# Moving the next chunk's transposes between the key and the query product in the input stage of an adaLN attention and experts kernel

## What is computed

```python
h = _layernorm(x, axis=-1) * (1 + ca) + sa
x = x + ga * attention(h, Wq, bq, Wk, bk, Wv, bv, Wo, bo)
h = _layernorm(x, axis=-1) * (1 + cb) + sb
x = x + gb * experts(h, gate_w, gate_b, W1, b1, W2, b2)
```

## Time and profile before

| what | us |
|---|---|
| median of 3 runs | 2086.68 (2086.62 to 2087.52) |
| the profiled execution's own time | 2084.18 |
| its span, first to last instruction | 2082.4 |
| first key product of the stage starts at | 40.30 |
| eighth key product starts at | 134.34 |
| last query store of the stage is issued at | 147.18 |
| first load of the next stage is issued at | 151.33 |

### The profile page before, as it was taken

One profiled execution on the slowest core, in us unless ns is written; L12 is line 12 of the kernel. 1 busy time (PEld: TensorE's weight loads), 2 busy tenths in 40 slices (PEclk: granted clock), 3 DMA queues, 4 the chain that ended last, 5 costly groups with the idle time before them and its releaser, 6 DMA issues. The chain is left out here.

```text
span 2082.4 us, 47224 instructions
## 1 busy us (share of the span) xinstructions
PE 1842.0 (88%) x18361; PEld 937.0 (45%) x18362; DVE 456.9 (22%) x1360; ACT 1327.4 (64%) x1633; POOL 290.1 (14%) x329
## 2 busy tenths in 40 slices
PE   4863899999999999999999999665499999999995
PEld 3542333333333333333333333554266676767674
DVE  4655000000000000000000000345233333333331
ACT  2432789998999989999899999222133333333331
POOL 1000110001100011100010000365121212121211
PEclk9995899999999999999999999666699999999998
DMA  4336320000400004000000000863412121221223
GB/s 136 121 130 138 58 60 10 10 10 17 80 17 10 9 18 80 18 10 10 10 25 10 17 2 2 313 222 124 137 33 33 33 33 33 33 34 32 34 32 97
DMA packets 83823, 116.06 MB, mean 56 GB/s; under 512 B 9372, under 2 KB 75612, under 8 KB 83036
## 3 DMA queue, kind: packets, MB, share of 16 engines
q1 hardware_dynamic: 66616, 90.97, 15.4%
q0 software_dynamic: 13296, 17.80, 5.0%
q10 hardware_dynamic: 3760, 5.03, 0.9%
HBM read 73.03 MB, written 40.74 MB: 55 GB/s over the span
## 5 line engine op out<-in xcount | busy, mean ns | idle before, releaser
L1063 ACT ACTIVATE at_probs<-at_scores 128x1536 f32<-128x1536 f32 (+2 forms) x756 | 1023.0, 1436 | 57.9 <-PE at_scores L965 52.7
L965 PE MATMUL at_scores<-at_q_rows,kept_k_rows 99*32 99x512 bf16 (+3 forms) x9920 | 618.6, 363 | 34.6 <-ACT at_probs L1063 17.0
L982 PE MATMUL at_out<-at_probs,kept_v 128*17 128x512 f32 (+3 forms) x4832 | 587.6, 566 | 5.0 <-DVE at_out_T L1076 5.0
L965 PEld LDWEIGHTS at_scores<-at_q_rows,kept_k_rows 99*32 99x32 bf16 x9920 | 238.4, 96 | 560.7 <-ACT at_probs L1063 343.3
L1770 ACT ACTIVATE ex_hT<-ex_ps_hT,kept_b 128x128 f32<-128x128 f32 x568 | 154.2, 383 | 375.9 <-PE ex_ps_hT L1727 375.9
L1716 PE MATMUL ex_ps_h<-kept_w,ex_xT 128*128 x568 | 260.1, 601 | 0.9 <-DVE ex_xT L1785 0.9
L1735 PE MATMUL ex_ps_y<-kept_w,ex_hT 128*128 x1136 | 258.7, 381 | 2.5 <-ACT ex_hT L1770 2.5
L1076 DVE COPY at_out_T<-at_out 128x512 f32<-128x512 f32 x32 | 22.1, 691 | 972.0 <-PE at_out L982 972.0
L1735 PEld LDWEIGHTS ex_ps_y<-kept_w,ex_hT 128*128 128x128 f32 x1136 | 211.5, 191 | 28.9 <-issue 2.7
L1048 POOL TENSOR_SCALAR_AFFINE_SELECT at_probs<-at_probs 128x512 f32<-128x512 f32 (+2 forms) x156 | 83.1, 541 | 1010.0 <-ACT at_probs L1063 1008.4
L982 PEld LDWEIGHTS at_out<-at_probs,kept_v 128*17 128x17 f32 x4832 | 127.2, 98 | 131.1 <-DVE at_out_T L1076 20.3
(11 more groups left out here) (206 smaller groups left out, 928.2 us busy)
## 6 DMA issues: line engine op xcount, KB each, us to landing
kept_w<-in_W SPq DMA_DIRECT2D x16, 1024.0 KB, 9.8
ex_x_tile<-queue SPq DMA_DIRECT2D x72, 129.5 KB, 2.0
k_parts<-kparts SPq DMA_DIRECT2D x8, 768.0 KB, 3.7
q_parts<-qparts SPq DMA_DIRECT2D x8, 768.0 KB, 3.7
at_q_rows<-q_parts SPq DMA_DIRECT2D x32, 192.0 KB
kept_k_rows<-k_parts SPq DMA_DIRECT2D x4, 1120.0 KB
x_rows<-in_x SPq DMA_DIRECT2D x4, 1024.0 KB, 14.0
kept_k_rows<-k_parts SPq DMA_DIRECT2D x8, 512.0 KB
```

The lines of the kernel that those rows point to most:

```text
L965: ins = nc.tensor.matmul(ps_s[b:b + CT, c % 2, at:at + part], k_rows[:, k + b:k + b + CT], q_rows[:, q:q + part], start=True, stop=True)
L982: ins = nc.tensor.matmul(ps_o[h * CT:h * CT + HD + 1, first:C], v[:, kb, g * GH + h, :], probs[:, slot, column:column + width], start=i == ...
L1063: nc.scalar.activation(probs[:, c % RING, 0:width], ps_s[:, c % 2, 0:width], ACT.Exp).then_inc(exped, 1)
```

## The change

All loops over chunks are written out, 8 chunks each, with constant addresses and constant semaphore values, and the `sem_inc` calls ahead of them go (waits that they served are left out for the first chunks instead). On TensorE a chunk's turning moves one chunk ahead: chunk c + 1 is turned between the key and the query product of chunk c. On ScalarE the modulation of chunk c + 1 and then the normalising of chunk c + 2 come between keeping the key product and keeping the query product of chunk c; ahead of the chunks stand the normalising of chunks 0 and 1 and the modulation of chunk 0. VectorE's and SP's orders stay. No buffer is added, and every instruction that computes is issued as often as before. The new text, cut to its core (the removed lines are those of the four loops printed above):

```diff
+            for c in range(NC):
+                u = c % 2
+                for n, (parts, name, kept) in enumerate(
+                        ((kparts, "k_parts", k_stored), (qparts, "q_parts", q_stored))):
+                    sp.wait_ge(parts_ready, 2 * c + n + 1)
...
+            def normalise(c):
+                u = c % 2
+                if c >= 2:
+                    act.wait_ge(turned, c - 1)
...
+            def modulate(c):
+                u = c % 2
+                if c >= 2:
+                    act.wait_ge(v_ready, c - 1)
+                act.wait_ge(turned, c + 1)
...
+            def keep_one(c, n, full, ps, scale, bias):
+                act.wait_ge(k_ready, 2 * c + n + 1)
+                if c > 0:
+                    act.wait_ge(parts_ready, 2 * c - 1 + n)
...
+            normalise(0)
+            normalise(1)
+            modulate(0)
+            for c in range(NC):
+                keep_one(c, 0, kf, ps_k, 1.0, bk)
+                if c + 1 < NC:
+                    modulate(c + 1)
+                if c + 2 < NC:
+                    normalise(c + 2)
+                keep_one(c, 1, qf, ps_q, HD ** -0.5, bq_scaled)
...
+            def turn(c):
+                u = c % 2
+                pe.wait_ge(xn_ready, (c + 1) * CB)
+                if c > 0:
+                    pe.wait_ge(h_ready, c * KD)
...
+            def project(c, n_out, w, ps):
+                u = c % 2
+                pe.wait_ge(h_ready, (c + 1) * KD)
+                if c > 0:
+                    pe.wait_ge(kq_kept, (2 * (c - 1) + n_out + 1) * KD)
...
+            def values(c):
+                u = c % 2
+                pe.wait_ge(h_ready, (c + 1) * KD)
+                if c > 0:
+                    pe.wait_ge(v_kept, c)
...
+            turn(0)
+            for c in range(NC):
+                project(c, 0, wk_turned, ps_k)
+                if c + 1 < NC:
+                    turn(c + 1)
+                project(c, 1, wq_turned, ps_q)
+                values(c)
...
+            for c in range(NC):
+                split(c, 0, kf, kparts, k_stored)
+                split(c, 1, qf, qparts, q_stored)
+                dve.wait_ge(v_ready, c + 1)
```

More of the change, by code:

```diff
@@ L182, in _ @@
                          ones_rows[:]).then_inc(ones_stored, 16)
[L183 to L191, removed]
+            for c in range(NC):
[3 more added lines that the diff above has]
+                    sp.wait_ge(parts_ready, 2 * c + n + 1)
+                    to = dram[name][0:PARTS, :, c * C:(c + 1) * C]
+                    sp.dma_start(to.rearrange("(a d) h s -> (d h) a s", a=3 * KD),
+                                 parts[:, u].rearrange("p a m s -> p (a m) s")).then_inc(kept[u], 16)
             sp.wait_ge(ones_stored, 16)
             for u in range(2):
-                sp.wait_ge(k_stored[u], 16 * (NC // 2 + 1))
-                sp.wait_ge(q_stored[u], 16 * (NC // 2 + 1))
+                sp.wait_ge(k_stored[u], 16 * (NC // 2))
+                sp.wait_ge(q_stored[u], 16 * (NC // 2))
         @block.gpsimd
@@ L246, in _ @@
             act.wait_ge(act_step, 3)
[L248 to L277, removed]
@@ new lines, in normalise @@
+            def normalise(c):
+                u = c % 2
+                if c >= 2:
+                    act.wait_ge(turned, c - 1)
+                for j in range(CB):
+                    t = c * CB + j
+                    nc.scalar.activation(xn[:, u, j, :], x[:, t, :], ACT.Identity, scale=rstd[:, t:t + 1],
+                                         bias=shift[:, t:t + 1]).then_inc(xn_ready, 1)
+            def modulate(c):
[3 more added lines that the diff above has]
+                act.wait_ge(turned, c + 1)
+                for k in range(KD):
+                    nc.scalar.activation(hT[:, u, k, :], ps_turn[:, k, :], ACT.Identity,
+                                         scale=mod_cols[:, 2 + k:3 + k],
+                                         bias=mod_cols[:, k:k + 1]).then_inc(h_ready, 1)
@@ new lines, in keep_one @@
+            def keep_one(c, n, full, ps, scale, bias):
+                act.wait_ge(k_ready, 2 * c + n + 1)
+                if c > 0:
+                    act.wait_ge(parts_ready, 2 * c - 1 + n)
+                for m in range(KD):
+                    nc.scalar.activation(full[:, m, :], ps[:, m, :], ACT.Identity, scale=scale,
+                                         bias=bias[:, m:m + 1]).then_inc(kq_kept, 1)
+            normalise(0)
[8 more added lines that the diff above has]
+                keep_one(c, 1, qf, ps_q, HD ** -0.5, bq_scaled)
@@ L297, in _ @@
             pe.wait_ge(w_in, 16 * 6)
[L298 to L305, removed]
-                    for k in range(KD):
[L307 to L325, removed]
@@ new lines, in turn @@
+            def turn(c):
[3 more added lines that the diff above has]
+                    pe.wait_ge(h_ready, c * KD)
+                for k in range(KD):
+                    for j in range(CB):
+                        last = nc.tensor.transpose(ps_turn[:, k, j * P:(j + 1) * P],
+                                                   xn[:, u, j, k * P:(k + 1) * P], ident[:])
+                last.then_inc(turned, 1)
+            def project(c, n_out, w, ps):
[3 more added lines that the diff above has]
+                    pe.wait_ge(kq_kept, (2 * (c - 1) + n_out + 1) * KD)
+                for m in range(KD):
+                    for k in range(KD):
+                        last = nc.tensor.matmul(ps[:, m, :], w[:, k, m * P:(m + 1) * P], hT[:, u, k, :],
+                                                start=k == 0, stop=k == KD - 1)
+                last.then_inc(k_ready, 1)
@@ new lines, in values @@
+            def values(c):
[3 more added lines that the diff above has]
+                    pe.wait_ge(v_kept, c)
+                for j in range(CB):
+                    for k in range(KD):
+                        last = nc.tensor.matmul(ps_v[:, j, :], hT[:, u, k, j * P:(j + 1) * P], wv[:, k, :],
+                                                start=k == 0, stop=k == KD - 1)
+                last.then_inc(v_ready, 1)
+            turn(0)
@@ L381, in _ @@
             dve.wait_ge(w_in, 16 * 6)
[L382 to L412, removed]
@@ L413, in _, with split @@
-            dve.wait_ge(v_kept, NC + 1)
+            def split(c, n, full, parts, kept):
+                u = c % 2
+                dve.wait_ge(kq_kept, (2 * c + n + 1) * KD)
+                if c >= 2:
+                    dve.wait_ge(kept[u], 16 * (c // 2))
+                step.inc(nc.vector.tensor_copy(parts[:, u, 0], full[:]))
+                step.wait(dve)
+                step.inc(nc.vector.tensor_tensor(full[:], full[:], parts[:, u, 0], ALU.subtract))
+                step.wait(dve)
+                step.inc(nc.vector.tensor_copy(parts[:, u, 1], full[:]))
+                step.wait(dve)
+                nc.vector.tensor_tensor(parts[:, u, 2], full[:], parts[:, u, 1],
+                                        ALU.subtract).then_inc(parts_ready, 1)
@@ new lines, in _ @@
+            rows = bv_rows[:].rearrange("p (h d) -> p h d", h=H)
+            for c in range(NC):
+                split(c, 0, kf, kparts, k_stored)
+                split(c, 1, qf, qparts, q_stored)
+                dve.wait_ge(v_ready, c + 1)
+                nc.vector.tensor_tensor(v[:, c * CB:(c + 1) * CB, :, 0:HD],
+                                        ps_v[:].rearrange("p j (h d) -> p j h d", h=H),
+                                        rows.unsqueeze(1).to_broadcast([P, CB, H, HD]),
+                                        ALU.add).then_inc(v_kept, 1)
@@ L415, in over_tiles @@
+            dve.wait_ge(v_kept, NC)
 def over_tiles(eng, body):
```

## The result

The changed kernel takes 2075.49 us (median of 6 runs, 2070.80 to 2077.33), the kernel before, measured beside it, 2087.65 (6 runs, 2086.62 to 2089.61). The ratio is 0.9938, 95% interval 0.9925 to 0.9951: between 10.2 and 15.7 us faster, 12.2 by the medians. The forecast of 14.7 lies inside that interval: by the medians 2.5 us are missing, and the runs don't separate that from nothing. The profiled execution took 2075.32, 8.86 under the profiled one of before, so this pair lacks 5.8 of the forecast. In the pair the stages can be compared one by one, and the question is where these 5.8 us went.

What follows compares the result with a forecast made beforehand. The first stage was taken as bound by TensorE and ScalarE waiting for each other once per chunk. Saving 14.2 us over seven boundaries plus 0.46 at entry, 14.7, took 2086.68 to 2072.0; range 2070.5 to 2078.5.

Steps and rivals of the forecast that it cites:

- The bound and the cycle: First stage: TensorE and ScalarE in lockstep; turning between key and query product cuts the cycle from 13.22 to 11.19 us.
- What must hide: First stage: ScalarE's late keep of q costs nothing; TensorE's waits are met with 3.9 us to spare, VectorE's with 1.3.
- The entry: Before the first stage's chunk loop: without loop set-up ScalarE starts normalising earlier, 0.46 us saved; other bound 0.
- the clock of the first chunk: First key product: an earlier start may shorten or lengthen its slow spell, plus or minus 1.6 us at most.
- the first boundary: Between the first two chunks of the first stage: saves the same as the other boundaries, 2.03 us.
- The loops: First stage: removing three back edges gives nothing, as cycles with and without one are both 13.22 us.
- the 7.2 us of three fetches: First stage's back edges: three code fetches of 2.4 us would go if taken branches forced them; left out of the sum.
- The code grows instead ... I take 0: TensorE's written-out first stage: 480 more instructions, two code fetches, taken as 0 us; upper bound 4.8.
- The end simply moves: End of the first stage: the chunk does the same after the last key product, so the end only comes earlier.
- signs of being wrong: Key products over 12.5 us apart, TensorE waiting on "issue" in the first stage, or later stages with other lengths.
- The rival of the loop pushed out of place: Expert loop: longer code ahead makes each of 35 passes pay a 2.4 us fetch, 84 us, 2156; chance 0.05.
- Fetching eats a third: Rival, first stage: two extra code fetches each stall TensorE, 4.8 us in all, time 2076.8; chance 0.08.

Runs made afterwards that it cites:

- the second: The changed kernel measured and profiled once more, unedited: 2073.87 us, ratio 0.9935 against the kernel before.

## Why the prediction was right, and what it missed

**The bound and the cycle: right.** The stage was a lockstep of TensorE and ScalarE, and the new cycle is 11.20 against 11.19 forecast, turning 0.87 against 0.88. The dense stream of the expert stage was the right row to take it from; the bound of 1.13 was not needed.

**What must hide: right.** No new wait for TensorE; VectorE waits 0.5 for q where 0.8 was counted. Keeping q ahead of normalising changes nothing clear of the noise.

**The entry: right.** 0.49 saved (0.58 less 0.09) against 0.46. But the step "the clock of the first chunk", kept only in the range, cost 0.4 in the first profile (5.39 against 5.02) and 1.6 in the second (6.59). So the first boundary did not save "the same": 1.56 (14.71 to 13.15) instead of 2.03.

**The loops: right.** Equal cycles across and within back edges said that removing these would give nothing; written out in the old order the time is 1.0004 of before, and the 7.2 us of three fetches that the prediction weighed and left out were not there to be had.

**The sum: off by what stood outside the stage.** The step that failed is "The code grows instead ... I take 0". The mechanism was named and priced (two stalls of 2.4 us at most), but looked for in the wrong place. The prediction looked for the extra fetches where the code was added, at 7 instructions per us, and there TensorE never waits on issue. It took attention's good record (22 fetches in 200 us, one stop) as evidence that fetching is safe, and did not ask why that one stop stood where it did: 13 us behind the issue of a load of 3.1 MB. Longer code ahead moves the border of every later block. Counted against the kernel before with its loads spread, the kernel before loses 4.4 + 0.7 us at its one stop; the changed kernel's two cost 7.6, 8.1 and 7.6 in the three profiles of its TensorE code, net 2.5 to 3.0 us. That is the traces' figure; the times are too noisy to confirm it, since spreading the loads gained 4.1 us on the changed kernel (2073.87 to 2069.78) and 3.4 on the kernel before, each uncertain by about 3.

"The end simply moves" assumes that later stages keep their lengths. One of the prediction's own signs of being wrong therefore came true: attention is 3.6 us longer in the profiled pair, mainly 2.5 by the stops and 1.3 by the clock at tile 8, which is that one execution's. Without stops in either kernel its length agrees within 0.3.

The rival of the loop pushed out of place had the right idea, code moved by an earlier edit, but at the wrong stage: the expert loops take 568.2 us as against 567.8. The rival "Fetching eats a third" had the right mechanism, longer code that stalls TensorE, with two stalls in the stage where there is one stop more in attention: the gain of 12.2 lies as near to its 9.9 as to the 14.7 of the forecast.

**Luck.** That the time lies in the range is in part luck. The range's room above was counted for fetches in the stage that never came, and nobody chose where the borders fell: in one session the same order on TensorE measured 2073.87, with its code moved by a loop 2081.22, and with the loads spread 2069.78.

The rule of the Trainium skill, Runtime: NRT & Kernel Launch, section "Instruction fetch mechanics", that code is refilled in blocks of 256 instructions agrees with the runs: 64 and 80 instructions more moved the stop by 192 and 177 records. Its remark that the cost of crossing a border is mostly hidden agrees with the rest of attention, where no stop over 1 us stands; behind a key load these runs show stops of 1.9 to 3.9 us.

Open: score_shifts took 3.2 us less in the changed kernel's first profile, and attention started no earlier for it; nor were the 1.2 us behind attention looked into. What decides whether the clock falls behind a stop is not shown. What the single executions of one kernel differ by (2081 to 2093 for the kernel before in one session) was not traced.

## What to carry to other kernels

An engine that waits once per chunk for the one that it feeds is freed by putting the next chunk's preparation between two independent products of this one; price the moved work by the same instructions in a dense stream, not by how long they take beside a gap. Code written out is moved code: everything behind it meets its block borders elsewhere, and a border that is reached 13 to 16 us behind the issue of a load of 3 MB stopped the engine here, so spread large loads that nobody needs yet. When a stage gains what it should and the total doesn't, align the two traces by an event that recurs to the end, and look for the one step in the differences.

## What the runs showed of the hardware

The profile counts TensorE's code among the packets of the same 16 DMA engines as data. With 3.1 MB issued ahead of it, a fetch that otherwise comes some 9 us behind the last came 17 to 20 us behind it, and the engine stood still for 1.9 to 3.9 us on "issue". The stops are at exact places in the code, 7400 records apart from group to group and the same in every profile of the same TensorE code, and 18 records' difference in place went with two stops instead of one.

What a stop costs depends on the clock behind it. At four of the 14 the granted clock stayed at 1.00, and attention lost 1.9 to 2.9 us, about the stop's own length of 1.9 to 2.9; at the other ten it fell to 0.50, and 3.6 to 6.0 us were lost (each counted at its tile and the next, against the kernel before with its loads spread).

A rest of 14 us cost TensorE about 1 us in the next eight transposes (1.94 against 1.04) and 1.5 to 3.1 us in the key product behind them (5.0 to 6.6 against 3.5); products that nobody reads, issued during the rest, take that away.
